# A routing stage written out in six uneven groups, with its logits taken from the projection

## The reference, cut to what matters

```python
h = h + attn(_layernorm(h))         # the mixer; its own residual is the normalised input
h = h + ffn(_layernorm(h))

def attn(x):                        # x: tokens of 192
    xn = gamma * (x / (rms(x) + 1e-6))
    xp = xn @ W_in.T + b_in         # 384 channels
    xc = conv(xp, conv_w)           # 4 taps along the sequence
    y = scan(sigmoid(A), sigmoid(Bp), sigmoid(C), xc)
    return y @ W_out.T + b_out + x

def ffn(x):
    logits = x @ Ws + bs            # 8 experts
    route, prob = argmax(softmax(logits)), max(softmax(logits))
    return prob * (gelu(x @ W1[route] + b1[route]) @ W2[route] + b2[route])
```

## Time and profile before

| | |
|---|---|
| median of 3 runs | 1388.22 us (1386.19 to 1389.48) |
| the profiled execution | 1383.82 us, of which the span from first to last instruction 1382.1 us |
| mean granted TensorE clock | 0.928 of full speed |
| busy share of the span | PE 84%, DVE 58%, ACT 50%, POOL 28% |
| DMA over the span | 133.83 MB, mean 97 GB/s |

### The profile page before, as it was taken

One profiled execution on the slowest core, in us unless ns is written; L12 is line 12 of the kernel. 1 busy time (PEld: TensorE's weight loads), 2 busy tenths in 40 slices (PEclk: granted clock), 3 DMA queues, 4 the chain that ended last, 5 costly groups with the idle time before them and its releaser, 6 DMA issues. The chain is left out here.

```text
span 1382.1 us, 38297 instructions
## 1 busy us (share of the span) xinstructions
PE 1162.4 (84%) x11847; PEld 1097.3 (79%) x11847; DVE 807.8 (58%) x2553; ACT 689.2 (50%) x1544; POOL 388.4 (28%) x358
## 2 busy tenths in 40 slices
PE   0398993565589999999999589995699999999998
PEld 0398893343479898898898389985699999999998
DVE  0778978873832633633536457777456556565664
ACT  2265662253752332232233246654577777777775
POOL 6877000002000300201202105546123333333332
PEclk9999997685789998998999889997899999999999
DMA  8866412005310322333233489992111111111110
GB/s 187 186 99 146 108 36 65 28 1 180 156 27 21 86 80 76 71 93 79 61 100 93 136 253 304 307 282 98 51 41 46 46 41 45 43 46 46 43 46 22
DMA packets 166427, 133.83 MB, mean 97 GB/s; under 512 B 77989, under 2 KB 155932, under 8 KB 164704
## 3 DMA queue, kind: packets, MB, share of 16 engines
q1 hardware_dynamic: 152352, 112.22, 30.2%
q0 software_dynamic: 10384, 17.49, 4.0%
q10 hardware_dynamic: 3600, 3.01, 0.8%
HBM read 89.97 MB, written 43.53 MB: 97 GB/s over the span
## 5 line engine op out<-in xcount | busy, mean ns | idle before, releaser
L2132 POOL DMA_INDIRECT out_dram<-ob,oi x89 | 127.0, 1427 | 283.4 <-DVE ob L2186 277.9
L2242 PE MATMUL ph<-zt,wc 64*128 64x128 f32 x3204 | 197.1, 274 | 3.0 <-issue 1.5
L2242 PEld LDWEIGHTS ph<-zt,wc 64*128 64x128 f32 x3204 | 191.7, 189 | 5.9 <-ACT zt L2144 2.9
L2234 PE MATMUL py<-w2c,ht 64*128 64x192 f32 x2136 | 194.1, 327 | 1.4 <-DVE yb L2184 1.4
L1499 PE MATMUL pa<-wi,xn 96*85 (+3 forms) x2048 | 186.9, 247 | 3.1 <-POOL mc L1351 2.9
L1499 PEld LDWEIGHTS pa<-wi,xn 96*85 96x85 f32 (+1 forms) x2048 | 181.4, 155 | 4.4 <-POOL mc L1351 3.1
L2157 ACT ACTIVATE ht<-ph,bc 128x128 f32<-128x128 f32 x534 | 156.5, 371 | 47.3 <-PE ph L2242 47.3
L2234 PEld LDWEIGHTS py<-w2c,ht 64*128 64x128 f32 x2136 | 172.7, 187 | 1.8 <-issue 1.3
L1362 POOL TENSOR_TENSOR bd<-rr,mc 128x656 f32<-128x656 f32 x48 | 61.5, 1282 | 309.0 <-PE pb L1517 188.0
L1373 DVE COPY x<-pa 85x384 f32<-85x384 f32 x100 | 55.4, 554 | 147.2 <-PE pa L1499 147.2
L341 PE MATMUL ps_y<-wg,xt 128*112 128x192 f32 x672 | 122.1, 333 | 13.4 <-DVE yg L431 13.4
(11 more groups left out here) (318 smaller groups left out, 1962.9 us busy)
## 6 DMA issues: line engine op xcount, KB each, us to landing
y<-yd SPq DMA_DIRECT2D x41, 384.0 KB, 4.8
gp<-kd SPq DMA_DIRECT2D x48, 246.0 KB, 2.8
xg<-in_x SPq DMA_DIRECT2D x16, 588.0 KB
xr<-xs SPq DMA_DIRECT2D x89, 98.0 KB, 1.9
yd<-yt SPq DMA_DIRECT2D x56, 144.0 KB, 1.9
hb<-h SPq DMA_DIRECT2D x41, 192.0 KB, 5.7
yd<-yt SPq DMA_DIRECT2D x40, 192.0 KB, 2.1
xg<-in_x SPq DMA_DIRECT2D x48, 112.0 KB
```

Source lines behind the costliest of these rows:

```text
L2132: pool.indirect_dma_start(out, bass.IndirectOffsetOnAxis(ap=oi[j][:, 0:1], axis=0), ob[j][:], None, bounds_check=bound, oob_is_err=False). ...
L2234: m = pe.matmul(py[h][:], ht[j][r, k, :], w2c[j % 2][r, k, :], start=(k == 0), stop=(k == FC - 1))
L2242: return pe.matmul(ph[c % 4][:, c // 4, :], wc[j][r, f:f + 128], zt[j][r, part, :], start=start, stop=stop, skip_group_check=True)
```

## The change

The logits come out of the projection. `wo` gets nine more columns (`DX` = 201): eight are the output weights times the router's centred weights, the ninth gives minus the row's mean. They are worked out in `embed_text`. The part of the logits that comes from the residual is added from `lgh`, which the mixer computes: `wi` gets eight more columns, the X units of block 0 (now `head_unit`, 104 columns, "H") yield them beside the input, two "L" units turn them, and the first instructions of `project_route` scale them. The transposes, the logits' products, the copies and the row statistics of `project_route` go; the variance comes from ScalarE (`squares`, one Square with a sum per token).

The loops of `project_route` go; the 41 pairs are written out, in groups of 3, 7, 9, 9, 8 and 5 pairs. Routing a group is placed at given pairs of the next (`STEPS`). There are still three row buffers, each for up to 18 tokens; GpSimd no longer waits for the group that it just sent, but for the one before that, and then gives back one buffer.

The weights of experts 0 to 3 are loaded in the last block of `mix` between the loads of the tables, those of expert 4 behind the ninth T unit's store, and those of 5 to 7 behind the last pair's loads. For that `xn` and the expert weights share one tile.

```diff
+NX = NEX + 1
+DX = D + NX
@@ embed_text: sync, vector, scalar, tensor
+                sp.dma_start(wsc[:, n, 0:NEX], io["L0_ffn_Ws"][n * HD:(n + 1) * HD, :]).then_inc(p_in, 16)
...
+            dve.wait_ge(p_turned, 1)
+            dve.memset(wsc[:, :, NEX:NX], -1.0 / D)
...
+                if m == 2:
+                    act.wait_ge(p_turned, 6)
+                    act.wait_ge(p_taken, 4)
+                    act.copy(wo[:, :, D:DX], po[1][:, 0, 0:KO * NX].rearrange("p (k e) -> p k e", e=NX))
+                    act.copy(keep["bow"][:], po[1][:, 1, 0:NX]).then_inc(p_taken, 1)
+                    act.copy(wi[0:HD, :, EB:EB + NEX], wsc[:, :, 0:NEX])
...
+                if m == 2:
+                    pe.wait_ge(w2_ready, 1)
+                    for k in range(KO):
+                        for q in range(2):
+                            pe.matmul(po[1][:, 0, k * NX:(k + 1) * NX], wout_row[:, q, k * 128:(k + 1) * 128],
+                                      wsc[:, q, :], start=(q == 0), stop=(q == 1))
...
+                    pe.wait_ge(p_taken, 5)
@@ mix: sync, the readers, tensor
+                    if last and g % 2 == 0:
+                        expert_weights(g // 2 - 2)
...
+                        if last and n == 8:
+                            expert_weights(EARLY_WEIGHTS - 1)
...
+            if kind == "H":
+                flat = p[0:W, :, :].rearrange("w a b -> w (a b)")[:, 0:4 * (EB + NEX)].rearrange("w (c e) -> w e c", c=4)
+                copy(lgx[:, :, 4 * n:4 * n + 4], flat[:, EB:, :])
+                copy(x[:, :, 4 * n:4 * n + 4], flat[:, 0:EB, :]).then_inc(free[who], 1)
+            elif kind == "L":
+                copy(keep["lgh"][:, 4 * n:4 * n + 4, :], p[:, :, HALO:W]).then_inc(free[who], 1)
...
             for m in range(XU):
-                input_unit(0, 0, m, m)
+                head_unit(m)
+            for n in range(LU):
+                p = bank(0, XU + n)
+                for who in range(2):
+                    pe.wait_ge(free[who], XU // 2 + 2)
+                for i in range(NEX // LU):
+                    tr = pe.transpose(p[:, i, 0:W], lgx[:, n * NEX // LU + i, :], ident[0:W, 0:W])
+                tr.then_inc(unit, 1)
@@ project_route
+ROUTED = (3, 7, 9, 9, 8, 5)
+        NR = 3
+        ROOT, EXPS = 2, 4
+        STEPS = [(0, 0, 1, 2)] * 2 + [(1, 2, 5, 6)] * (NGR - 2)
+        def due(p, which):
+            for g in range(1, NGR):
+                if P0[g] + STEPS[g][which] == p or (p == NP and P0[g] + STEPS[g][which] >= NP):
+                    return g - 1
+            return None
+        def place(p):
+            g = max(g for g in range(NGR) if P0[g] <= p)
+            return g, 2 * (p - P0[g])
...
+            for p in range(NP):
+                q = p % PG
+                if p >= PG:
+                    sp.wait_ge(h_done, p - PG + 1)
+                sp.dma_start(yt[q][:], ydv[:, :, Q - 2 - 2 * p:Q - 2 * p, :]).then_inc(y_in[q], 16)
+                sp.dma_start(hb[q][:], hv[:, 2 * p:2 * p + 2, 0:D]).then_inc(y_in[q], 16)
+            for e in range(EARLY_WEIGHTS, NEX):
+                load_expert(sp, io, late, wl, e)
...
-                if reused:
-                    pool.wait_ge(sent, 16 * TG * g + 16 * n)
-                    hold(pool, row_free)
...
+            for g in range(NGR):
+                pool.wait_ge(rows_ok, g + 1)
+                for t in range(2 * ROUTED[g]):
+                    pool.indirect_dma_start(dr["xs"], bass.IndirectOffsetOnAxis(ap=sli[g % NR][:, t:t + 1], axis=0),
                                            row[g % NR][:, t, :], None, bounds_check=bound, oob_is_err=False
                                            ).then_inc(sent[g % 2], 16)
+                if g:
+                    landed(g - 1)
+                    pool.sem_inc(row_free, 1)
+            landed(NGR - 1)
...
+            def squares(p):
+                g, c = place(p)
+                act.wait_ge(h_done, p + 1)
+                if p >= 2:
+                    act.wait_ge(sq_ok, p - 1)
+                for t in (c, c + 1):
+                    a = act.activation(sq[2 * (p % 2) + t % 2][:], row[g % NR][:, t, 0:D], ACT.Square, bias=lgs[g % NR][:, t, NEX:NX],
+                                       accum_out=var[g % 2][:, t:t + 1])
+                a.then_inc(sq_ok, 1)
...
+            LAG = 3
+            for p in range(NP):
+                residual(p)
+                if p >= LAG:
+                    squares(p - LAG)
+                for g in range(1, NGR):
+                    if p == P0[g] + ROOT:
+                        root_of(g - 1)
+                    if p == P0[g] + EXPS:
+                        exp_of(g - 1)
...
+                    for k in range(KO):
+                        m = pe.matmul(po[q][:, i, 0:DX], yt[q][:, k, 1 - i, :], keep["wo"][:, k, :],
+                                      start=(k == 0), stop=(k == KO - 1))
...
+            for p in range(NP + 1):
+                if p < NP:
+                    project(p)
...
+                if due(p, 3) is not None:
+                    rank(due(p, 3))
...
+            def finish(p):
+                q = p % PG
+                g, t = place(p)
                 dve.wait_ge(hb_ok, p + 1)
                 tt(hb[q][:], hb[q][:], bo[:, :].unsqueeze(1).to_broadcast([CB, 2, D]), ALU.add).then_inc(biased, 1)
+                dve.wait_ge(out_ok, p + 1)
+                if g >= NR and t == 0:
+                    dve.wait_ge(row_free, g - NR + 1)
+                tt(lgs[g % NR][:, t:t + 2, :], po[q][:, :, D:DX], lgh[:, :, 2 * p:2 * p + 2].rearrange("c e t -> c t e"),
+                   ALU.add)
                 dve.wait_ge(biased, p + 1)
+                tt(row[g % NR][:, t:t + 2, 0:D], hb[q][:], po[q][:, :, 0:D], ALU.add).then_inc(h_done, 1)
...
+            def route1(g):
+                n = 2 * ROUTED[g]
+                dve.wait_ge(sq_ok, P0[g + 1])
+                ts(sd[:, 0:n], var[g % 2][:, 0:n], 1.0 / D, EPS, ALU.mult, ALU.add).then_inc(var_ok, 1)
+                ts(row[g % NR][:, 0:n, D], lgs[g % NR][:, 0:n, NEX], -1.0, None, ALU.mult)
...
+            for p in range(NP + 1):
+                if p < NP:
+                    finish(p)
...
+                for which, stage in enumerate((route1, route2, route3)):
+                    if due(p, which) is not None:
+                        stage(due(p, which))
+            route1(NGR - 1)
+            route2(NGR - 1)
+            route3(NGR - 1)
```

More of the change, by code:

```diff
@@ L860, in _ @@
             sums(0, HB)
-            pe.wait_ge(p_in, 80)
+            pe.wait_ge(p_in, 144)
+            for k in range(2):
+                t = pe.matmul(po[0][0:HD, 0, 0:NEX], keep["ones"][0:HD, 0:HD], wsc[:, k, 0:NEX], start=(k == 0), stop=(k == 1))
+            t.then_inc(p_turned, 1)
             for k in range(2):
@@ L1057, in normalise_in @@
         vv = sb("vv4", [CB, 2, Q])
-        zs = sb("zs4", [CB, Q])
+        zs = keep["zs"]
         nz = sb("nz4", [CB, Q])
@@ L1232 @@
 XU = CB // 4
+LU = 2
 IU = EB // 4
@@ L1499, in input_unit, with head_unit @@
                         mm = pe.matmul(p[:, i * EB:(i + 1) * EB], xn[0:rows, f, b, c * Q:c * Q + W],
-                                       keep["wi"][0:rows, f, bass.ds(k * EB, EB)],
+                                       keep["wi"][0:rows, f, bass.ds(k * EB + NEX, EB)],
                                        start=(f == 0), stop=(f == 1))
+                mm.then_inc(unit, 1)
+            def head_unit(m):
+                p = bank(0, m)[0:W, :, :].rearrange("w a b -> w (a b)")
+                for c in range(NCHUNK):
+                    for f in range(2):
+                        rows = HD + f
+                        mm = pe.matmul(p[:, c * (EB + NEX):(c + 1) * (EB + NEX)], xn[0:rows, f, m, c * Q:c * Q + W],
+                                       keep["wi"][0:rows, f, 0:EB + NEX], start=(f == 0), stop=(f == 1))
                 mm.then_inc(unit, 1)
@@ L1677, in project_route @@
         mu, rs = keep["mu"], keep["rs"]
-        w1, w2, b1, b2 = late["w1"], late["w2"], late["b1"], late["b2"]
-        def groups(eng, body):
-            body(0, 0, True)
-            with eng.Fori(0, NFULL // 3) as i:
-                for a in range(1, 4):
-                    body(3 * i + a, a % 3, False)
+        b1, b2 = late["b1"], late["b2"]
         def empty_rows(eng, experts):
@@ L1817, in _ @@
+            for p in range(NP - LAG, NP):
+                squares(p)
+            root_of(NGR - 1)
+            exp_of(NGR - 1)
             empty_rows(act, range(NEX // 2, NEX))
@@ L1871, in _ @@
-            pe.wait_ge(iot, 5)
-            pe.wait_ge(w_in, 80)
-            for k in range(2):
-                pe.matmul(pc[0:HD, :], ones[0:HD, 0:HD], ws[:, k, :], start=(k == 0), stop=(k == 1))
-            pe.transpose(pb1[:, :], b1row[:], ident[0:NEX * FC, 0:NEX * FC]).then_inc(wsum, 1)
-            pe.sem_inc(zt_ok, 2)
-            pe.sem_inc(l_taken, 3)
-            pe.wait_ge(tab_ok, 1)
-            groups(pe, body)
```

(2 more changed lines are left out.)

433 lines of the change are left out of this document (163 added, 270 removed).

## The result

The changed kernel takes 1393.32 us (median of 20 runs) beside 1388.33 us for the kernel before (20 runs): a ratio of 1.0034, 95% interval 1.0018 to 1.0051. It is slower, as forecast, but by 5 us and not by 33: 1421 was forecast. One of the 20 runs, 1492.94 us at a granted clock of 0.798, is left out of the ratio. The profiled execution is a long one, 1401.29 us with a span of 1399.5, and that of the kernel before a short one, 1383.82. A stage is counted from its first GpSimd instruction in the timeline to the next one's; within the mixer the marks are the groups' `bd` products.

The account below looks back on a forecast made before the run. GpSimd's scatters, 1.28 us each, were taken to set the routing stage's pace. Terms 21 + 2 + 2 + 2 + 3.5 + 2.2 = 32.7 us on 1383.8 gave 1416.5, plus 4.4 for the runs' median 1421; range 1386 to 1442.

Parts of the forecast that it names:

- The wait that the change adds: Routing stage: VectorE waits for row buffers, three turns (last issue to next first scatter) of 16 us; last scatter 21 later.
- the buffer's wait costs nothing: Rival, routing stage: VectorE gets the buffer before pair 19; last issue 22 us sooner, total 1378; chance 0.14.
- The other steps of the stage: Routing stage: first scatter at +31, group 1 at +56, 1.28 us a scatter, weights of experts 5 to 7 free.
- Weights in the mixer's last block: Mixer's last block: table loads behind four experts' weights come up to 4 us late; 2 us in all, at most 6.
- The T units: Mixer's end: expert 4's weights between the T units' stores delay the following store; 3.5 us, between 1 and 5.
- The mixer's head: Block 0: 104 for 96 columns cost 2 us, the transposes and a read before the first I unit 2.0 us.
- The text stage: Text stage, turn 2: more small products and a wait for ScalarE's copies; 2.2 us, between 0.5 and 4.5.
- The experts: Expert stage, from the last scatter's start to the end: no term in the sum, forecast difference 0.
- The sign: Whole kernel: slower 0.82, same 0.04, faster 0.14.
- The rule of the Trainium skill: Routing turns: matmul bursts between waits start cold, so each of three turns costs 17.3 us, the stage 4 us more.

Follow-up runs that it names:

- the second profile: Profile of the changed kernel run again unedited, span 1394.8 us; that run measured 1395.8 us, ratio 1.0024 to the kernel before.
- free_landed: Changed kernel, but GpSimd gives a row buffer back only when all scatters of the group just issued have landed: 1437.1 us, ratio 1.0364.
- weights_late: Changed kernel, but none of the experts' weights is loaded in the mixer; all eight follow the routing stage's last pair loads: 1377.0 us, ratio 0.9948.
- dve_pad: Kernel with all weights late and in tiles of their own, plus 128 unused semaphore instructions on VectorE's queue behind the mixer: 1388.1 us, ratio 1.0001.
- L_last: Changed kernel with the two units transposing the router's columns moved behind the mixer's last T unit: 1398.4 us, ratio 1.0098.

## Why the prediction was wrong

**The wait that the change adds** is the step that failed: "`row_free` for that buffer is given only after GpSimd has issued the whole of group 1". It was given when twelve of the group's scatters had yet to run, some 15 us of cover (12 x 1.28) for a turn of 16. Three turns of 16 us became gaps of 4.1, 0 and 0 (4.1, 2.2 and 0 in the second profile). This is in effect the rival "the buffer's wait costs nothing", forecast at -22 and measured at -18; but the condition named for it, scatters of 0.5 us, was the wrong one, since they still start 1.28 apart. The evidence against it, a period read from engine time, says nothing of when the queue goes past. `free_landed` shows that the rest of the step held for the first two turns; the third was priced 4 us too dear, since only five pairs are left there.

**The other steps of the stage** held: first scatter +32.9 (+31), group 1 +58.3 (+56), the pace 1.28, experts 5 to 7 at no cost.

**Weights in the mixer's last block** was mis-sized: 2 us, at most 6, and measured 8.3. The issue time of a following table, 3.04 for 0.53 us, was left out, and with a table 6 us late TensorE's granted clock fell to 0.59. The T units: 3.5, measured 6.1, beyond the bound of 5. `weights_late` shows that both are the weights' doing.

**The mixer's head** took 4.1 to 5.7 us more in nine profiles, for a forecast 4; in the profile of the result half clock added 4.

**The text stage**: 2.2 was forecast between 0.5 and 4.5; the ten profiles lie 0.3 to 5.9 above before.

**The experts** were put at nothing in the sum, without a reason, and lost 4 to 7 us: VectorE's queue no longer hides what it does at the end of its loop's turn. Why it lost its lead is open: the shared tile explains about 2 us, a shift of the code (`dve_pad`) decides nothing.

The sign came out right by luck, by two errors that pull against each other: the stage 39 us too dear, the rest 19 us too cheap by the second profile and 11 by the medians.

The rule of the Trainium skill that the prediction weighed, "TensorE: Matmul & The Clock Gate", section "HAM oscillation — how this bites in real kernels", spoke of turns that did not come. In `free_landed`, where they come, the clock falls in them and two take 16.8 and 17.2 us, nearer to the 17.3 by that rule than to the 14.5 of a warm engine.

## What to carry to other kernels

A semaphore instruction behind indirect DMAs on GpSimd is not behind their execution: look up in the trace when its line ran, not when the engine's bar ends. Loads that are moved "to where the queues are light" are paid by the next small load on the same queue; leave them behind the last load that anyone waits for, if the stage still has tens of us to run. When code is written out or moved, look also at stages that the diff does not touch: a loop's jump there may come to cost more, and the period by tile shows it.

## What the runs showed that was not expected

GpSimd's queue goes past 11 to 12 scatters that have not run. The jump back of TensorE's block loop costs 2.4 to 3.1 us in thirteen profiles and 6.2 and 6.5 in `L_last`, by where the code lies, and eighteen idle instructions decide between them. An idle semaphore instruction on VectorE is not free either: 128 of them ran for 12.1 us and made the mixer's end 9.7 us longer. Two short pauses of TensorE, of about 1 us each, were followed by half clock in one execution and by full clock in another of the same kernel.
